# A gated linear-attention and FP4 block on one core: flux network's inner values by unit, modulation gates in rows of four partitions, step lists placed anew

## The reference, cut to what matters

```python
mod = (_silu(L0_c) @ L0_wmod).reshape(4, 6, 1, -1)
sa, ca, ga, sb, cb, gb = (mod[:, 0], ..., mod[:, 5])
ga = (2 * (ga >= 0) - 1) * jnp.maximum(jnp.abs(ga), 0.25)
gb = (2 * (gb >= 0) - 1) * jnp.maximum(jnp.abs(gb), 0.25)
h = _layernorm(x) * (1 + ca) + sa
x = x + ga * attention(h)
h = _layernorm(x) * (1 + cb) + sb
x = x + gb * fp4_ffn(h)      # 128 -> 2 x 352 -> 128

# in attention, for each head (b h l d), d = 8
q, k = l2norm(h @ Wq), l2norm(h @ Wk);  v = h @ Wv
k_beta = k * sigmoid(h @ Wb)
hmid = silu(k_beta @ Wtf1 + btf1)                    # 4 inner units
flux = clip(sigmoid(hmid @ Wtf2 + btf2), 0.01, 0.99)
# decays: fast_w, slow_w = exp of suffix sums of log decays
# M = (k_beta * w)^T v_scaled / sum(w);  o = alpha*q@M_fast + (1-alpha)*q@M_slow
```

## Time and profile before

| what | value |
|---|---|
| timed runs, median (lowest, highest) | 210.43 us (210.26, 210.82) |
| profiled execution, its span | 209.9 us |
| busy: PE, DVE, POOL, ACT | 184.1, 174.6, 152.7, 144.9 us |
| table loads on ACT | 10, 1.28 us each |

### The profile page before, as it was taken

The page is one execution under the profiler, slowest core; times in us unless marked ns, Lnnn a source line. Parts: engine busy times, 40 slices in busy tenths (PEclk is TensorE's granted clock), DMA queues, the critical chain, the costliest instruction groups (busy, mean ns, idle before and its releaser), DMA issues.

```text
span 209.9 us, 3498 instructions
## 1 busy us (share of the span) xinstructions
PE 184.1 (88%) x948; PEld 134.0 (64%) x948; DVE 174.6 (83%) x436; ACT 144.9 (69%) x326; POOL 152.7 (73%) x187
## 2 busy tenths in 40 slices
...
PEclk9999999699999999999999999999999999999999
...
DMA packets 11499, 5.66 MB, mean 27 GB/s; under 512 B 1684, under 2 KB 11352, under 8 KB 11480
## 3 DMA queue, kind: packets, MB, share of 16 engines
...
q10 hardware_dynamic: 312, 0.13, 0.2%
...
## 4 chain that ended last, share of the span: by engine, by line
PE 54%; ACT 15%; issue 12%; POOL 9%; DVE 6%; DMA 2%; SPq 0%; POOLq 0%; ACTq 0%; DVEq 0%
PE pa L1089 11%; PE pa L1166 6%; PE pg L1113 5%; PE pv L1168 5%; PE pa L1190 5%; PE pv L1130 4%; POOL q_o L487 3%; POOL q_r L475 3%; PE pa L1177 3%; PE pa L1139 3%; DMA wmod_sb<-in_L_wmod_dram 2%; ACT xn L680 2%; PE pv L1149 2%; ACT L526 2%; PE pa L1185 2%
## 5 line engine op out<-in xcount | busy, mean ns | idle before, releaser
L475 POOL TENSOR_TENSOR q_r<-q_x,q_rs 128x960 f32<-128x960 f32 (+2 forms) x18 | 29.6, 1645 | 14.3 <-DVE q_rs L960 14.3
L1089 PE MATMUL pa<-wcat,hT 128*128 128x496 f32 x64 | 31.5, 620 | 5.6 <-ACT sq L606 3.4
L487 POOL TENSOR_TENSOR q_o<-q_r,q_sp 128x960 f32<-128x960 f32 (+2 forms) x18 | 29.6, 1644 | 7.2 <-DVE q_r L971 6.4
L1166 PE MATMUL pa<-guT,hqT 128*128 128x352 f32 x64 | 25.3, 477 | 4.8 <-ACT hqT L697 4.7
L1190 PE MATMUL pa<-wdg,fqT 128*128 128x128 f32 x192 | 26.9, 276 | 0.0
L706 ACT ACTIVATE sgl<-pa 128x352 f32<-128x352 f32 x32 | 14.5, 461 | 15.1 <-PE pa L1166 12.8
L1168 PE MATMUL pv<-guT,hqT 128*128 128x352 f32 x64 | 24.3, 462 | 0.3 <-DVE oc L913 0.3
L438 POOL TENSOR_TENSOR vs<-kvg,cw 128x256 f32<-128x256 f32 x32 | 20.2, 658 | 5.7 <-DVE cw L864 5.7
L1190 PEld LDWEIGHTS pa<-wdg,fqT 128*128 128x128 f32 x192 | 24.0, 192 | 0.4 <-ACT fqT L714 0.2
L1089 PEld LDWEIGHTS pa<-wcat,hT 128*128 128x128 f32 x64 | 12.0, 204 | 16.6 <-ACT sq L606 6.8
L691 ACT ACTIVATE q_A<-q_r 128x960 f32<-128x960 bf16 (+2 forms) x18 | 16.0, 888 | 8.5 <-POOL q_r L475 5.3
...
## 6 DMA issues: line engine op xcount, KB each, us to landing
...
```

Of the source, the lines that this page charges most:

```text
L475: g.tensor_tensor(blocks(q_r[:, s % 2, c]), blocks(q_x[:, s % 2, c]), spread(q_rs[:, s % 2, n]), ALU.mult)\
L487: g.tensor_tensor(blocks(q_o[:, s % 2, c]), blocks(q_r[:, s % 2, c]), spread(q_sp[:, s % 2, n]), ALU.mult)\
L1089: te.matmul(bank_a(("PP%d" % k, i))[:, 0:NCAT], hT[:, b, 2 * j + k, :], wcat[:, :], start=True, stop=True).then_inc(S["a_full"], 1)
L1166: te.matmul(bank_a(("G%d" % k, i))[:, 0:I], lhs, guT[:, 0, :], start=True, stop=True)\
```

## The change

Three things, in one diff.

1. The inner values of the flux network lie unit by unit. `bd1` and with it the 64 extra columns of `wcat` are ordered unit first; `hin` and `hmid` become [partition, unit, tile, head], so that each of the 4 silu instructions on ACT and each of the 4 `hz` instructions on DVE reads 128 adjacent values. Counts and sizes of instructions stay.
2. The modulation gates are worked on as rows. A new PE step `MR` multiplies silu(c) as the stationary operand (4 columns) with `wmod`: 4 partitions (one for each batch) of 512 values, in a `pv` bank. A new DVE step `MR` does add-one, sign and floor on those 4 partitions, in 5 instructions. `MB` then spreads the finished rows with a stationary operand of one identity column, repeated (4 x 128), in 4 products of 512 columns as before. `SB` (one copy, 128x512) and `W0` (9 instructions, 128x512) are gone. Whoever waited for `W0` (semaphore `mbe`) now waits for ACT's last copy of `MB`.
3. The four lists in `ORDER` are written anew (a name `dma:0` in ACT's list has no function and does nothing).

```diff
-        CT:0 WK:0 CM:0 PX:0 PX:1 KW:0 PX:2 PX:3 PP:0 PP:1 PP:2 PX:4 PP:3 PX:5 MB:0 PX:6 PP:4 PX:7 WQ:0 GA:0 PP:5
+        CT:0 dma:0 WK:0 WQ:0 CM:0 KW:0 PX:0 PX:1 PX:2 PP:0 PP:1 PX:3 PP:2 PX:4 PP:3 PX:5 GA:0 PP:4 PP:5 PX:6
...
-        bd1 = sb("bd1", [P, H, HM])
+        bd1 = sb("bd1", [P, HM, H])
...
-        scB = sb("scB", [P, NB, P])
+        mrow = sb("mrow", [NB, 4, D])
...
-        hin = sb("hin", [P, T, H, HM])
-        hmid = sb("hmid", [P, T, H, HM])
+        hin = sb("hin", [P, HM, T, H])
+        hmid = sb("hmid", [P, HM, T, H])
...
-                g.tensor_tensor(hin[:, :, :, :], gates(b, 3 * H, NG).rearrange("p t (h j) -> p t h j", j=HM),
-                                kb[:, :, :].unsqueeze(3).to_broadcast([P, T, H, HM]), ALU.mult).then_inc(S["hin0"], 1)
+                g.tensor_tensor(hin[:, :, :, :], gates(b, 3 * H, NG).rearrange("p t (j h) -> p j t h", j=HM),
+                                kb[:, :, :].unsqueeze(1).to_broadcast([P, HM, T, H]), ALU.mult).then_inc(S["hin0"], 1)
...
-                    a.activation(hmid[:, :, :, j], hin[:, :, :, j], ACT.Silu, bias=btf1_b[:, j:j + 1]).then_inc(S["hmid"], 1)
+                    a.activation(hmid[:, j], hin[:, j], ACT.Silu, bias=btf1_b[:, j:j + 1]).then_inc(S["hmid"], 1)
...
-            def W0(_):
-
-                dve.wait_ge(S["a_free"], slot_a[("MB%d" % (NB - 1), 0)] + 1)
-                v.tensor_scalar(mb[:, :, 2, :], mb[:, :, 2, :], 1.0, None, ALU.add).then_inc(S["mbe"], 1)
...
+            def MR(_):
+
+                t = bank(("MR", 0))[0:NB, :].rearrange("b (m d) -> b m d", m=4)
+                v.tensor_scalar(mrow_s[:, :, :], t[:, 0:4:3, :], 0.0, 0.5, ALU.is_ge, ALU.subtract).then_inc(S["mrow"], 1)
+                v.tensor_copy(mrow[:, 1, :], t[:, 1, :]).then_inc(S["mrow"], 1)
+                v.tensor_scalar(mrow[:, 2, :], t[:, 2, :], 1.0, None, ALU.add).then_inc(S["mrow"], 1)
+                dve.wait_ge(S["mrow"], 3)
+                v.scalar_tensor_tensor(mrow_a[:, :, :], mrow_s[:, :, :], 4.0, t[:, 0:4:3, :], ALU.mult, ALU.mult)\
+                    .then_inc(S["v_free"], 1)
+                dve.wait_ge(S["v_free"], slot_v[("MR", 0)] + 1)
+                v.scalar_tensor_tensor(mrow[:, 0:4:3, :], mrow_a[:, :, :], 0.5, mrow_s[:, :, :], ALU.max, ALU.mult)\
+                    .then_inc(S["mrow"], 1)
...
-                    v.scalar_tensor_tensor(hz[:, :, :], hmid[:, :, :, j], wtf2_b[:, j:j + 1], hz[:, :, :],
+                    v.scalar_tensor_tensor(hz[:, :, :], hmid[:, j], wtf2_b[:, j:j + 1], hz[:, :, :],
...
+            def MR(_):
+                a_done(("CT", 0))
+                pe.wait_ge(S["wmod"], 16)
+                te.matmul(bank_v(("MR", 0))[0:NB, :], scT[:, :], wmod_sb[:, 2 * D:6 * D], start=True, stop=True)\
+                    .then_inc(S["v_full"], 1)
+
             def MB(_):
-                pe.wait_ge(S["scB"], 1)
-                pe.wait_ge(S["wmod"], 16)
+                v_done(("MR", 0))
+                pe.wait_ge(S["mrow"], 4)
                 for b in range(NB):
-                    te.matmul(bank_a(("MB%d" % b, 0))[:, :], scB[:, b, :], wmod_sb[:, 2 * D:6 * D],
-                              start=True, stop=True).then_inc(S["a_full"], 1)
+                    te.matmul(bank_a(("MB%d" % b, 0))[:, :], ident[0:NB, b:b + 1].to_broadcast([NB, P]),
+                              mrow[:, :, :].rearrange("b m d -> b (m d)"), start=True, stop=True).then_inc(S["a_full"], 1)
```

108 lines of the change are left out of this document (48 added, 60 removed).

## The result

| | before | after |
|---|---|---|
| median of the runs | 210.62 us (210.26 to 210.82, 4 runs) | 225.38 us (222.59 to 225.9, 4 runs) |
| span of the profiled execution | 209.9 us | 224.1 us |
| mean granted clock | 0.992 | 0.962 |
| start of the first feed-forward product | 76.61 us | 84.14 us |

The changed kernel is slower: its time is 1.0613 of that before, 95% interval 1.0548 to 1.0678. The forecast was 207.0, in a range of 204.4 to 211.0. Executions of one kernel differ, and the ratio on record answers to a time of before of about 212, not to 210.62 (225.38 / 210.62 would be 1.070): of 43 more runs of the kernel before, the 10 with a mean granted clock of 1.0 took 210.1 to 211.0 us, and the 33 with 0.984 to 0.992 took 211.6 to 213.4.

The account below looks back on a forecast made before the run. The prediction took each stage to be bound by the engine waited for, with DVE fullest from 76.6 to 179.6. Terms -0.3 - 1.1 - 1.2 - 0.8 = -3.4 gave span 206.5, plus 0.5 a median of 207.0, range 204.4 to 211.0.

Parts of the forecast that it names:

- Lists: 2.6 us of PE work moved ahead of the first feed-forward product, taken from behind it: a shift, costed at nothing.
- rival 3: Behind the first feed-forward product a chain of sixteen rounds, not work, sets the length: 212.2 or 210.4 us; chance 0.16.
- Clock, -1.2: If PE's second gap shrinks, the dip to 1.2 GHz behind it need not come: -1.2 us, bounds 0 and -1.6.
- Start, -0.3: First projection behind three transposing steps instead of four, `MV` and `KW` moved ahead: -0.3 us, bounds 0 and -0.5.
- The first gap: PE's 2.66 us wait while ACT is in `GA:0`; `MR`'s 0.9 us product falls into it and costs nothing.
- `MR` on DVE, 1.7 us: The 5 DVE instructions in place of `W0` take 1.7 us, between 1.5 and 3.0.
- Is the row ready?: Whether DVE's `MR` ends before PE reaches `MB`: 8.9 us against 9.4 from the start of `GA:0`, so no cost.
- `MB` in the second gap, -1.1: `MB` moves behind `GE:0` into PE's 2.21 us gap and fills half: -1.1 us, bounds 0 and -2.2.
- Silu, 0: ACT's silu on adjacent values drops from 526 to 396 ns, 0.5 us for each batch; taken as nothing.
- `hz`, -0.8: Batch 3's four DVE `hz` instructions, on adjacent values, fall from 2.0 to 1.1 us: -0.8; 0 if POOL holds them up.
- the first product later than 77.5: Sign of being wrong: the first feed-forward product was expected at about 76.6 us.
- a stage behind it that is not shorter than 133 us: Sign of being wrong: from the first feed-forward product to the end, some 130 us were expected.

Follow-up runs that it names:

- e5: The changed kernel with the lists of before and `MB`'s products taken from 128 partitions instead of 4; 213.01 us, ratio 1.0017 to before.
- e8: The changed kernel with `MB` on 128 partitions, new lists up to the first feed-forward step and the lists of before behind it; 214.38 us, ratio 1.0089.
- e2: The changed kernel, new lists kept, with `MB`'s products taken from 128 partitions instead of 4; 220.32 us, ratio 1.0418 to before.
- e1: The changed kernel with the lists of before, `MB` still on 4 partitions; 215.0 us, ratio 1.0136 to before.
- e10: e2 with the start of the PE, ACT and DVE lists (`WQ`, `KW`, `MV`, `P0:1`) put back as before; 221.11 us, ratio 1.0442 to before.
- e9: e2 with the small product `nmrb` of each pair moved from DVE to three ACT instructions; 221.62 us, ratio 1.0454 to before.
- e3: The kernel before with the unit-by-unit layout of the inner values alone; 211.24 us, ratio 0.997 to before.

## Why the prediction was wrong

**The step that failed first is "Lists: ... While work bounds that stage, this is a shift: nothing".** By the ratios of e5, e8 and e2 the lists cost 8.5 of the 13.0 us that 1.0613 stands for: 7.0 behind the first feed-forward product, clear of noise, and 1.5 at the head, which is not. Two things were wrong in the step.

- The 2.6 us of PE's work moved ahead were not given back. From the first feed-forward product to the end it is 133.3 us before, 133.3 in e1 (213.0 - 79.67) and 133.6 in e8 (212.6 - 79.01), although e8 has this work ahead of it (e8's dip in that stage, 3.4 us at one half, can hide some 1.7 of the 2.6 by my estimate, half of its length). That is the mechanism of rival 3, a chain of rounds, to which I gave 0.16. "Against it: DVE is 93% busy" was no argument: a DVE that stands under POOL counts as busy, and the chain of before runs through DVE for 6% of the span and through PE for 54.
- Behind it the order was costed by its work, not by who stands beside whom. The new one puts DVE's small instructions under POOL's of 1.8 us: 7.3 us of DVE's busy time, and 27% of the chain instead of 10. I had the row for this and the rule, and used them for one term, `hz`, and not for the lists.

**Clock, -1.2: "the dip need not come"** is the second step that failed. At 4 partitions the clock fell: +5.1 in the first profile, +2.4 in the second, 4.1 by the ratios with the new lists, 2.5 with the old. "`MB` has the same size, 3.7 us on PE" was right at full clock (3.67) and wrong in the profile of after (5.98). No row of before shows a product of many columns from few partitions, so the bound from the rows (0 to -1.6) left out a loss; it should have been open upwards. And the term had little to win. A run's time is 1.7 to 1.8 us above its span in all 43 more runs of before, not 0.5: the profiled execution, span 209.9 with a dip, answers to 211.6, and the timed runs of 210.26 to 210.82 look like those at a mean clock of 1.0, which have no dip to give back.

**Start, -0.3.** The sign was wrong. The first projection starts at 10.10, not ahead of 9.69: PE waits 1.11 for Wq's transfer and 0.37 for the third pair's `xn`, and the clock rises at 14.0 where it was 10.7 before. Undone in e10 it gave 1.25 us up to the first gap, and nothing at the end.

**The first gap, `MR` on PE, 0.9 for nothing.** Right: 1.02 us ahead of a gap of 2.14. **`MR` on DVE, 1.7 us.** Right: from 28.10 to 29.78. **Is the row ready?** Nearly: PE waited 0.21, and `MB` starts at 29.89, 0.11 behind the end of the row; in e9 and e10, where the row is done at 27.93 and 28.45, there is no such wait. **`MB` in the second gap, -1.1.** The mechanism was right: `MB` stands where the gap of 2.21 was, behind waits of 0.31 and 0.21, and PE's idle time from the first projection to the first feed-forward product fell from 5.63 (66.90 with 61.27 busy) to 4.68 (74.00 with 69.32 busy), -1.0. But its busy time in the same stretch rose by 8.05, of which `MR` and the steps moved ahead are 3.6 at most (1.0 and 2.6); that the low clock is most of the rest is my estimate, from 10.2 us of it in this profile and 3.4 in that of before.

**Silu, 0.** Its size was right (392 ns for 396 forecast). What it brings, with `hz` and the rest of the layout, is 1.9 us by the first feed-forward product in the profile of e3, and in its runs nothing that can be told from no change (0.9922 to 1.0018); part of the 1.9 is the dip of the clock from 38.0 that e3's profile doesn't have.

**`hz`, -0.8.** Failed; it is 0. The instructions take 595 ns on average after (552 before), and 550 in e3. The row and rule against the term decided it: with both inputs in SBUF they wait for POOL, wherever the values lie. Of the 12 in the profile of after, 11 end 0.14 to 0.15 us behind the end of a POOL instruction (104.96 behind 104.81); the one with none beside it takes 0.35.

Of the signs that I had named as showing me wrong, two came: the first product later than 77.5, and a stage behind it that is not shorter than 133 us (224.1 - 84.14 = 140.0). The third, PE standing before `MB`, came with 0.21 us.
